# The last feed-forward of a two-layer graph network, on all rows or on the chosen 1561 rows

## The reference

```python
def _L1_ffn_ref(x, attention_mask, wr, br, w1, b1, w2, b2):
    CAPACITY = 0.5
    b, s, d = x.shape           
    weights = (jnp.einsum('bsd,do->bso', x, wr) + br)[..., 0]
    k = max(1, int(CAPACITY * s))
    kk = k - 1 if k > 1 else 1   
    _, idx = jax.lax.top_k(weights, k)
    sel_idx = idx[:, :kk]
    sel = jnp.take_along_axis(x, sel_idx[:, :, None], axis=1)
    h = jax.nn.gelu(jnp.einsum('bkd,dh->bkh', sel, w1) + b1)
    y = jnp.einsum('bkh,hd->bkd', h, w2) + b2 
    w_sel = jnp.take_along_axis(weights, sel_idx, axis=1)
    y = y * w_sel[..., None]
    processed = jnp.zeros_like(x).at[batch_idx, sel_idx].set(y)
    return processed + x
...
x = x + _L1_ffn_ref(_layernorm(x, axis=-1)[None], ...)[0]
```

## Time and profile before

| | |
|---|---|
| median of 3 runs | 2247.16 us (2247.13 to 2251.39) |
| the profiled execution | 2252.55 us |
| its span on the core | 2250.8 us |
| PE busy | 1764.1 us (78%) |
| DVE busy | 1300.4 us (58%) |
| POOL busy | 1116.5 us (50%) |
| ACT busy | 595.4 us (26%) |
| DMA mean | 102 GB/s |

### The profile page before, as it was taken

One profiled execution on the slowest core, in us unless ns is written; L12 is line 12 of the kernel. 1 busy time (PEld: TensorE's weight loads), 2 busy tenths in 40 slices (PEclk: granted clock), 3 DMA queues, 4 the chain that ended last, 5 costly groups with the idle time before them and its releaser, 6 DMA issues. The chain is left out here.

```text
span 2250.8 us, 25718 instructions
## 1 busy us (share of the span) xinstructions
PE 1764.1 (78%) x8446; PEld 1034.2 (46%) x8446; DVE 1300.4 (58%) x2672; ACT 595.4 (26%) x940; POOL 1116.5 (50%) x888
## 2 busy tenths in 40 slices
PE   7984554544553869999999619799989999997996
PEld 6962222222222654555554418655565565544543
DVE  6878866776764457777777404645541231125996
ACT  4001111110110136666666211312120010003453
POOL 0768787887875868888888767000000000000344
PEclk9557787867775559999999757899999999997998
DMA  6347788878876212221210200344325433521002
GB/s 173 85 135 197 213 225 217 226 220 219 226 204 165 57 30 45 35 34 34 34 34 5 68 1 2 63 102 107 93 60 130 127 83 100 129 70 38 1 4 82
DMA packets 193284, 229.07 MB, mean 102 GB/s; under 512 B 66688, under 2 KB 174292, under 8 KB 187811
## 3 DMA queue, kind: packets, MB, share of 16 engines
q1 hardware_dynamic: 126001, 172.58, 29.1%
q0 software_dynamic: 67200, 55.46, 11.1%
HBM read 148.81 MB, written 78.24 MB: 101 GB/s over the span
## 5 line engine op out<-in xcount | busy, mean ns | idle before, releaser
L715 POOL DMA_INDIRECT adjacency<-all_cell_val,all_cell_idx x400 | 519.4, 1299 | 151.9 <-issue 120.9
L281 POOL DMA_INDIRECT edge_ring<-b_rows,all_src_idx x400 | 493.9, 1235 | 186.8 <-issue 169.4
L1755 POOL TENSOR_TENSOR ffn_hl<-ffn_hid,ffn_hh 128x448 f16<-128x448 f32 x56 | 70.2, 1256 | 742.6 <-ACT ffn_hid L1772 742.5
L1568 PE MATMUL bank<-sage_adj,sage_zh 125*128 125x448 f16 x1050 | 370.1, 352 | 3.4 <-DVE sage_zl L1622 3.4
L1568 PE MATMUL bank<-sage_adj,sage_zl 125*128 125x448 f16 x1050 | 370.0, 352 | 0.0
L535 DVE SCALAR_TENSOR_TENSOR edge_ring<-edge_ring,w_keep 125x256 f32<-125x256 f32 x399 | 192.9, 483 | 128.8 <-DMA edge_ring<-b_rows,all_src_idx 109.0
L1214 ACT ACTIVATE bank<-bank,w_shift,w_scale 128x448 f32<-128x448 f32 x224 | 147.1, 697 | 76.7 <-PE bank L728 69.8
L1645 DVE TENSOR_TENSOR sage_u<-bank,w_rd 128x448 f32<-128x448 f32 x42 | 26.2, 624 | 236.2 <-PE bank L1573 233.4
L1568 PEld LDWEIGHTS bank<-sage_adj,sage_zh 125*128 125x128 f16 x1050 | 102.6, 98 | 101.8 <-issue 8.0
L1568 PEld LDWEIGHTS bank<-sage_adj,sage_zl 125*128 125x128 f16 x1050 | 102.7, 98 | 99.7 <-issue 5.8
L690 DVE SCALAR_TENSOR_TENSOR edge_junk<-bank,all_key_c,all_later 125x400 f16<-125x400 f32 x232 | 145.4, 627 | 0.0
(11 more groups left out here) (435 smaller groups left out, 3474.9 us busy)
## 6 DMA issues: line engine op xcount, KB each, us to landing
sage_adj<-adjacency SPq DMA_DIRECT2D x105, 490.0 KB
run_max<-edge_ring SPq DMA_DIRECT2D x40, 1120.0 KB
adjacency<-edge_zero SPq DMA_DIRECT2D x25, 714.0 KB
experts_gb<-gate_rows SPq DMA_DIRECT2D x56, 224.0 KB
edge_ring<-b_rows,all_src_idx POOLq DMA_INDIRECT x400
adjacency<-all_cell_val,all_cell_idx POOLq DMA_INDIRECT x400
sage_adj<-adjacency SPq DMA_DIRECT2D x105, 56.9 KB
run_max<-edge_ring SPq DMA_DIRECT2D x40, 130.0 KB
```

The source lines that it names most:

```text
L281: nc.gpsimd.indirect_dma_start(ring[:, k % RING, :], None, dram.rows[:, :], bass.IndirectOffsetOnAxis(ap=c.src_idx[:, k:k + 1], axis=0)).t ...
L715: nc.gpsimd.indirect_dma_start(dram.adj_flat, bass.IndirectOffsetOnAxis(ap=c.cell_idx[:, k:k + 1], axis=0), c.cell_val[:, k:k + 1], None). ...
L1568: ins = mm(ps[4 * b + h][:, 0:T], z[:, g * JG + j, half(h)], adj[g][:, j, :], start=(g == 0 and j == 0 and z is zh), stop=False)
L1755: nc.gpsimd.tensor_tensor(hl[:, m, :], hid[:, m, :], hh[:, m, :], ALU.subtract).then_inc(low, 1)
```

## The change

- `sage` gets an argument `tail`, given for layer 2 only. The 7 tiles are then written out instead of looped. When PE has done two of the five groups of a tile, it transposes the 3 or 4 finished row blocks of the tile before into PSUM (`rows(t - 1)`); DVE norms them there in row form (mean and variance by BN_STATS and BN_AGGR, deviation by ACT), makes x + norm(x) and the score, and SP stores each block twice: `[norm, x + norm, score]`, 513 numbers a row, to a new DRAM tensor `x_rows`, and x + norm(x) to the output. `norm` number 3 and `split_weights` are gone as stages; the weights are loaded and split inside this `sage`.
- `ffn1` is replaced by `ffn_chosen`. The 1561st largest score is found bit by bit: the score's 32 bits in eight digits (one of 3 bits, then seven of 4), where DVE compares all scores with 7 or 15 candidates, sums along the row, and PE sums over partitions with a product with ones. Places within the chosen set come from a product with a triangular matrix and a scan; node numbers are brought into 13 columns of 125 (`SLOTS`) by 25 small products of one-hot matrices.
- POOL then gathers 13 x 125 rows of `x_rows` by indirect DMA. PE transposes them, and the feed-forward runs on groups of 1, 4, 4 and 4 slots (125 or 500 rows), `up` in 8 blocks of 128 hidden rows, `down` with the rows on the output's partitions. DVE adds the bias, multiplies by the score and adds x + norm(x); POOL scatters each finished slot to the output by indirect DMA.

Cut to its core (`...` where lines are left out). The pieces are, in this order: SP's stores and loads in `sage`; PE's transposes there and their place in a tile; DVE's `rows`; then `ffn_chosen` with its sizes, DVE's loop over the digits, DVE's order of `lows` and `finish`, PE's products and their order, POOL's gathers, and POOL's subtractions and scatters.

```diff
-def sage(nc, c, w, dram, layer, fold, extra, mix=None):
+def sage(nc, c, w, dram, layer, fold, extra, mix=None, tail=None):
...
+                def store_rows(t):
+                    j, n = ROWS[t]
+                    sp.wait_ge(row_ready, t + 1)
+                    for p in HALVES:
+                        for to, from_ in ((dram.rows2, rr[p, 0:n, :]), (tail.out, rr[p, 0:n, D:2 * D])):
+                            sp.dma_start(to[B * j:B * (j + n), :].rearrange("(i p) f -> p i f", p=B)[p], from_).then_inc(tail.stored[t % 2], 16)
...
+                for t in range(1, NT):
                     for g in range(SG):
                         sp.wait_ge(adj_used, SG * (t - 1) + g + 1)
                         load(t, g)
+                    if t >= 2:
+                        store_rows(t - 2)
+                store_rows(NT - 2)
+                store_rows(NT - 1)
...
+                def rows(t):
+                    j, n = ROWS[t]
+                    pe.wait_ge(own, DVE_N * (t + 1) + 1)
+                    if t:
+                        pe.wait_ge(row_ready, t)
+                    for i in range(n):
+                        for h in range(KH):
+                            ins = nc.tensor.transpose(bank(i)[:, half(h)], c.xT[:, h, B * (j + i):B * (j + i + 1)], c.ident[:])
+                    ins.then_inc(row_turned, 1)
...
                     for g in range(SG):
+                        if tail and g == 2 and t:
+                            rows(t - 1)
                         pe.wait_ge(adj_in[g], 32 * t + 32)
...
+                def rows(t):
+                    j, n = ROWS[t]
+                    dve.wait_ge(row_turned, t + 1)
+                    if t:
+                        dve.wait_ge(tail.stored[(t - 1) % 2], 64 * ((t - 1) // 2 + 1))
+                    for i in range(n):
+                        ins = v.bn_stats(stats[:, i, :], bank(i))
+                    rstep(ins)
+                    for i in range(n):
+                        ins = v.bn_aggr(mv[:, i, :], stats[:, i, :])
+                    ins.then_inc(row_var, 1)
+                    dve.wait_ge(row_dev, t + 1)
+                    dve.wait_ge(row_var, t + 1)
+                    rstep(v.reciprocal(rs[:, 0:n], dev[:, 0:n]))
+                    for i in range(n):
+                        ins = v.tensor_scalar(rr[:, i, 0:D], bank(i), mv[:, i, 0:1], rs[:, i:i + 1], ALU.subtract, ALU.mult)
+                    rstep(ins)
+                    for i in range(n):
+                        v.tensor_tensor(rr[:, i, D:2 * D], rr[:, i, 0:D], bank(i), ALU.add)
+                    for i in range(n):
+                        ins = v.scalar_tensor_tensor(junk[:], rr[:, i, 0:D], 1.0, tail.wr[:], ALU.mult, ALU.mult, accum_out=raw[:, i:i + 1])
+                        rstep(ins)
...
+def ffn_chosen(nc, c, tail, dram, out):
     M1 = HID1 // P
+    SLOTS = -(-TOPK // B)
+    REST = TOPK - B * (SLOTS - 1)
+    GROUPS = [(0, 1)] + [(k, min(4, SLOTS - k)) for k in range(1, SLOTS, 4)]
+    TURN_AT = lambda g: 2 if g else M1 - 1
...
+                for n, (shift, k) in enumerate(DIGITS):
+                    step(v.tensor_tensor(cand[:, 0:k], tail.digits[:, n, 0:k], pre[:].to_broadcast([B, k]), ALU.bitwise_or))
+                    step(v.tensor_tensor(over[:, 0:k, :], flip[:].unsqueeze(1).to_broadcast([B, k, NB]),
+                                         cand[:, 0:k].bitcast(F32).unsqueeze(2).to_broadcast([B, k, NB]), ALU.is_ge))
+                    v.tensor_reduce(part[:, 0:k], over[:, 0:k, :], AX.X, ALU.add).then_inc(parts, 1)
+                    step(v.tensor_scalar(junk[:, 0:k], total(n + 1)[:, 0:k], want[:, 0:1], None, ALU.is_ge, ALU.add, accum_out=digit[:]))
+                    step(v.tensor_scalar(more[:], digit[:], float(1 << shift), None, ALU.mult))
+                    step(v.tensor_tensor(pre[:], pre[:], more[:], ALU.bitwise_or))
...
+                lows(0)
+                for g, (first, n) in enumerate(GROUPS):
+                    if g + 1 < len(GROUPS):
+                        lows(g + 1)
+                    for k in range(first, first + n):
+                        finish(k)
...
+                def up(g, m):
+                    n = M1 * g + m
+                    if m == 0:
+                        pe.wait_ge(x_low, g + 1)
+                    if n >= 4:
+                        pe.wait_ge(g1, n - 3)
+                    product3(nc, ps[n % 4][:, 0:wide(g)], [(tail.w1[0][:, k * HID1 + m * P:k * HID1 + (m + 1) * P], tail.w1[1][:, k * HID1 + m * P:k * HID1 + (m + 1) * P]) for k in range(KH)],
+                             [(xh[:, k, at(g)], xl[:, k, at(g)]) for k in range(KH)]).then_inc(f1, 1)
...
+                def down(g, i):
+                    k = GROUPS[g][0] + i
+                    pe.wait_ge(low, M1 * (g + 1))
+                    if k >= 2:
+                        pe.wait_ge(evacuated, k - 1)
+                    tok = slice(B * i, B * (i + 1))
+                    product3(nc, ps[4 + k % 2][0:B, 0:D], [(hh[:, g % 2, m, tok], hl[:, g % 2, m, tok]) for m in range(M1)],
+                             [(tail.w2[0][:, m * D:(m + 1) * D], tail.w2[1][:, m * D:(m + 1) * D]) for m in range(M1)]).then_inc(f2, 1)
...
+                turn(0)
+                for g in range(len(GROUPS) + 1):
+                    for m in range(M1):
+                        if g < len(GROUPS):
+                            up(g, m)
+                        if m == TURN_AT(g) and g + 1 < len(GROUPS):
+                            turn(g + 1)
+                        if g and m % 2 == 1 and m // 2 < GROUPS[g - 1][1]:
+                            down(g - 1, m // 2)
...
+                for k in range(SLOTS):
+                    nc.gpsimd.indirect_dma_start(rows[:, k, :], None, dram.rows2[:, :],
+                                                 bass.IndirectOffsetOnAxis(ap=idx[:, k:k + 1], axis=0)).then_inc(got[k], 16)
...
+                for g, (first, n) in enumerate(GROUPS):
+                    for m in range(M1):
+                        pool.wait_ge(g1, M1 * g + m + 1)
+                        if g >= 2:
+                            pool.wait_ge(f2, GROUPS[g - 2][0] + GROUPS[g - 2][1])
+                        nc.gpsimd.tensor_tensor(hl[:, g % 2, m, 0:wide(g)], hid[:, m, 0:wide(g)], hh[:, g % 2, m, 0:wide(g)], ALU.subtract).then_inc(low, 1)
+                    if g:
+                        for k in range(GROUPS[g - 1][0], GROUPS[g - 1][0] + GROUPS[g - 1][1]):
+                            place(k)
+                for k in range(first, first + n):
+                    place(k)
```

379 lines of the change are left out of this document (200 added, 179 removed).

## The result

The changed kernel takes 2180.72 us (median of 4 runs, 2178.27 to 2182.23) against 2247.14 us: ratio 0.970, 95% interval 0.968 to 0.972, **66.4 us faster**. The forecast was 2169, the range 2156 to 2192. The profiled execution took 2178.27 us on the device, with a span of 2176.4.

A forecast was written before the change was run, and what follows sets the result against it. PE was taken to bound the last convolution and, with DVE's ranking beside it, the feed-forward. Nine terms summed to 148.8 us in place of 227.6, 78.8 us less, giving a forecast of 2169 us, range 2156 to 2192.

The forecast's parts named there:

- a dearer search: Rival: digit search and places cost half as much again; +17 us, 2186 us; chance 0.15.
- GpSimd as the bound: Rival: GpSimd's work, slowed beside DVE's, bounds the feed-forward; +7 us, 2176 us; chance 0.13.
- (a): Transposes inside the last convolution: 42 at 0.133 us, 5.6 us, all on the path; the stores hidden.
- (b): Rows of the last tile: transposes, norm, x + norm and score behind the convolution, 9.0 us.
- (d): Digit search for the threshold score: seven digits at 2.65 us, a short one and a sign pass, 23.0 us.
- (e): Places and node numbers behind the search, up to the indices: 10.5 us.
- (c): SP's last four stores and the barrier before the search: 1.6 us of stores, 3.0 us in all.
- (f): Gathers on POOL: 2.2 us for the first, then twelve at 1.52, 20.5 us; POOL's queue sets this, not landing.
- (g): POOL's eight subtractions of 125 columns for the first group, behind the gathers: 3.3 us.
- (h): PE's feed-forward from `down(0, 0)` on, with 2.4 us of waiting and a 2 us restart: 68.3 us.
- (i): The end: last `finish` 1.0, a scatter 1.5, landing and last barrier 1.54 + 1.5; 5.6 us.
- PE was at half clock in the feed-forward: Rival: PE stays at half clock through the feed-forward because stalls keep coming; up to +60 us, 2229 us; chance 0.05.

The follow-up runs named there:

- e9: Changed kernel without 30 of the 42 transposes in the last convolution's tiles (output wrong); trace only: six tiles took 132.94 us instead of 136.21.
- e8: Changed kernel with the search stopped after four of its eight digits (output wrong); trace only: the search took 12.28 us instead of 23.0.
- e1: Changed kernel with the last tile's four stores issued in the feed-forward's stage; 2185.59 us, ratio 0.969 to the kernel before.
- e2: Changed kernel with group 0's eight subtractions moved from GpSimd to VectorE; 2180.85 us, ratio 0.9682 to the kernel before.
- e7: Changed kernel with only nine slots of rows in the feed-forward (output wrong); trace only: first to last `finish` 39.96 us instead of 63.88.
- e3: Changed kernel with VectorE making the next group's low halves after a group's first `finish`, not ahead of its finishes; 2184.93 us, ratio 0.9706 to the kernel before.
- c0: Changed kernel run again without an edit; 2186.05 us beside 2252.43 of the kernel before, ratio 0.9706.
- e6: Changed kernel with the last 61 rows stored plainly by SP instead of scattered (output wrong); trace only: the end took 7.33 us instead of 11.57.
- e4: Changed kernel with the 61-row slot taken first, so the last scatter has 125 rows; 2178.65 us beside 2248.61 of the kernel before, ratio 0.9687.

## Why the prediction was right, and what it missed

The direction and the mechanism were right, and the size nearly so, since the sum was made of rows: six of nine terms came within 0.2 us of the trace, a seventh within 1.0. But 2180.72 lies above the band that the prediction gave its own forecast, 2160 to 2176. It is inside the range only because the range had room for two rivals, a dearer search and GpSimd as the bound, and neither of them happened; that the range held is in part luck.

- **(a)** 42 at 0.133 was 1.0 too much. The row it came from the earlier trace rows had 18 transposes with hand-overs among them; e9 gives 0.109 each.
- **(b), (d), (e)** were right: 9.2, 23.0, 10.4. In (b) two parts were off and cancelled: subtract and multiply, read from PSUM, took 1.90 instead of 1.38 us, and the four score products 0.47 each instead of 0.56. A bit operation on integers takes 0.16 to 0.17 us, as any small step, so the rival of the dearer search (0.15) falls. That a digit is one chain with no cover is what e8 shows.
- **(c) is one of the two steps that failed.** "SP's last four stores 1.6 us" took 0.40 us for each issue, the price at the end of the kernel before, where stores of one row block (112.0 or 13.0 KB) are issued one by one. Here four blocks are stored at once. The first two issues, with 1345.8 KB, took 0.31 and 0.49 us; the two small ones behind them 1.74 and 1.89, while the DMA engines worked off what was queued at a share of 1.00. So the size of a store does not set its issue. What fits is that an issue waits for room behind the stores ahead of it, as the expectation of e1 had it; no run emptied the queue to show it. e1: 4.8 us for these issues instead of 1.6, and 1.7 for the barrier instead of 1.4, inside the 0.92 to 1.86 that the earlier trace rows had. The same price stood in (a) for the stores of each tile; there issues of up to 2.27 us did no harm, since they were hidden.
- **(f)** The sum held (20.4), but two parts of it were off and cancelled. The first gather took 1.23 us on GpSimd and not 2.20, behind a start 0.98 us late. The landing, taken as 2 us from its issue, was 5.45 (2073.85 to 2079.30), still under the 8 us from which it would decide `down(0, 0)`. That GpSimd's queue sets it was right, and e2 and e7 confirm it.
- **(g), (h)** were right in sum (3.2 and 68.4). `lows(3)` behind `finish(4)` costs the forecast 2.4 us (e3: 2.4). The restart of 2 us was there as well: `down(0, 0)` took 4.46 us at clock 0.62 where 24 matmuls at 0.109 would be 2.6. That the 2 us fitted was luck: in the kernels in which GpSimd still subtracts for group 0, `down(0, 0)` took from 2.87 us (c0) to 5.42 (e6), and another 1.6 us came and went behind `up(3, 0)`. The prediction did not say that the clock does this from one execution to the next.
- **(i) is the other step that failed.** "A scatter 1.5, its landing and the last barrier 1.54 + 1.5" took a plain store's landing for a scatter's, and an ordinary barrier for the close of a stage in which GpSimd issued 26 DMAs. Behind GpSimd's 1.67 us the landing took 4.7 us instead of 1.54, and what followed it 3.9 instead of 1.5. Of the 6.0 us missed, 2.5 are the 61 rows on one DMA engine (e4), some 1 is that a scatter of 125 rows, too, lands 2.6 us behind GpSimd's instruction, and 2.2 are GpSimd's DRAIN (e6).

The misses sum to 8.5 us, 157.3 instead of 148.8. That makes 2169 into 2177.5. The other 3 us are not in the region: the span of before was compared through one profiled execution, and the time up to the first tile varies by 10 us between executions (1886.55 in that one, 1882.5 to 1892.4 in the others). Which execution is typical one trace of before can't tell. The traces say that the region became 70.3 us shorter (72.0 in c0), the runs 66.4 both times; whether the changed program is also slower ahead of the region stays open.

The rivals: GpSimd as the bound was refuted by e7 and by the spacing of 5.16; its subtractions of 500 columns took 1.13 us. PE was at half clock in the feed-forward in three stretches (2079.3 to 2083.8, 2090.7 to 2093.7, 2097.5 to 2100.9), 10.9 us together. That is more than the 5 us which the prediction had named as a sign against it, but far from all of it: from 2100.9 to 2165 the clock was 1.00. Stores that starve the loads were refuted by e9. That the rows multiplied would not be fewer was excluded: 13 slots at 5.16 us.
